# Local attention on one Trainium2 core: turning and weighing of the probabilities moved one unit behind the scores, exponentials taken from PSUM with the maximum as bias

## The reference

```
def _layer(x, wqkv, qs, ksc, wo, lg, lb, w1, b1, w2, b2):
    h = shift_token(x)
    qkv = h @ wqkv
    q, k, v = jnp.split(qkv, 3, axis=-1)
    ...
    q = l2norm(q) * qs
    k = l2norm(k) * ksc
    q, k = rotary_xpos(q, k)
    o = local_attention(q, k, v)      # softmax(q k^T * 8 + mask) v, over own and previous window
    ...
    x = x + o @ wo
    h = shift_token(x)
    ...                               # layer norm of h
    h = h @ w1 + b1
    a, g = jnp.split(h, 2, axis=-1)
    h = a * jax.nn.gelu(g, approximate=False)
    x = x + h @ w2 + b2
    return x
```

## Time and profile before

| what | us |
|---|---|
| three timed runs | 1561.47, 1565.78, 1570.25 (median 1565.78) |
| the profiled execution, its own time | 1563.58 |
| its span, first to last instruction | 1561.7 |
| steady attention of layer 0, of layer 1 (about) | 750 to 1017, 1167 to 1433 |
| busy PE, DVE, ACT, POOL | 1346.8, 1145.6, 801.7, 724.0 |

### The profile page before, as it was taken

One profiled execution on the slowest core, in us unless ns is written; L12 is line 12 of the kernel. 1 busy time (PEld: TensorE's weight loads), 2 busy tenths in 40 slices (PEclk: granted clock), 3 DMA queues, 4 the chain that ended last, 5 costly groups with the idle time before them and its releaser, 6 DMA issues.

```text
span 1561.7 us, 39029 instructions
## 1 busy us (share of the span) xinstructions
PE 1346.8 (86%) x15968; PEld 970.4 (62%) x15968; DVE 1145.6 (73%) x2484; ACT 801.7 (51%) x1633; POOL 724.0 (46%) x562
## 2 busy tenths in 40 slices
PE   4545999988999999984999999967989999998797
PEld 3434878875777777762666666654556666665554
DVE  3776776434888888874888888864578888888565
ACT  1222223224666666653777777742457777776421
POOL 1752545541344433434666666632246666666100
PEclk7776999996999999997999999999999999999999
DMA  4000544500000000003000100011100000000011
GB/s 133 0 0 16 112 93 110 108 13 2 3 3 3 4 3 3 3 3 91 8 8 7 22 8 8 1 30 28 25 24 8 9 17 13 9 5 2 12 31 54
DMA packets 61837, 40.34 MB, mean 26 GB/s; under 512 B 41312, under 2 KB 51808, under 8 KB 61664
## 3 DMA queue, kind: packets, MB, share of 16 engines
q1 hardware_dynamic: 61664, 37.88, 10.2%
HBM read 27.12 MB, written 2.36 MB: 19 GB/s over the span
## 4 chain that ended last, share of the span: by engine, by line
PE 33%; ACT 8%; SPq 6%; DVE 4%; POOL 2%; issue 1%; DMA 1%; DVEq 0%; POOLq 0%; ACTq 0%
PE PS L1872 7%; SPq L1463 5%; PE PS L1923 5%; PE PS L1957 4%; PE PS L1914 4%; PE PS L1891 3%; PE PS L1937 2%; ACT e_oT L1787 2%; PE PS L1948 2%; ACT qk L1756 2%; ACT e_pm L1793 2%; PE PS L1907 2%; POOL rot L1537 2%; PE PS L2010 1%; PE PS L2019 1%
## 5 line engine op out<-in xcount | busy, mean ns | idle before, releaser
L1537 POOL TENSOR_TENSOR rot<-qk,sinl 128x1024 f32<-128x1024 f32 x64 | 217.6, 3401 | 139.4 <-DVE qk L1631 139.4
L1530 POOL TENSOR_TENSOR rn<-ss,neghalf 128x16 f32<-128x16 f32 x64 | 185.6, 2901 | 108.6 <-DVE ss L1624 108.6
L1756 ACT ACTIVATE qk<-PS 128x512 f32<-128x512 f32 x128 | 76.4, 597 | 135.7 <-PE PS L1872 135.7
L1102 DVE TENSOR_REDUCE d_mx<-PS 128x4 f32<-128x576 f32 x128 | 96.9, 757 | 66.3 <-PE PS L1246 63.3
L1872 PE MATMUL PS<-wqkv,hT 128*128 128x512 f32 x256 | 128.8, 626 | 10.9 <-DMA qks<-in_e_ks 5.7
L607 POOL TENSOR_TENSOR uu<-uu,cb 128x512 f32<-128x512 f32 x64 | 82.8, 1295 | 90.0 <-DVE uu L839 88.2
L1923 PE MATMUL PS<-ident,e_pm 128*128 128x128 f32 x512 | 84.5, 289 | 45.9 <-ACT e_pm L1793 44.3
L1923 PEld LDWEIGHTS PS<-ident,e_pm 128*128 128x128 f32 x512 | 55.9, 144 | 102.4 <-ACT e_pm L1793 95.7
L739 ACT ACTIVATE sg<-PS 128x512 f32<-128x512 f32 x72 | 43.0, 597 | 134.1 <-PE PS L667 133.0
L1165 ACT ACTIVATE pa<-PS 128x512 f32<-128x512 f32 x128 | 76.5, 597 | 61.8 <-PE PS L1255 61.7
L1610 DVE TENSOR_REDUCE e_mx<-PS 128x8 f32<-128x1024 f32 x64 | 78.2, 1222 | 30.7 <-PE PS L1914 30.6
(11 more groups left out here) (241 smaller groups left out, 3535.9 us busy)
## 6 DMA issues: line engine op xcount, KB each, us to landing
cb<-comb_rows SPq DMA_DIRECT2D x32, 512.0 KB, 9.1
X<-in_L_attn_x SPq DMA_DIRECT2D x4, 512.0 KB, 7.4
zs<-Z SPq DMA_DIRECT2D x64, 32.0 KB
zg<-Z SPq DMA_DIRECT2D x16, 128.0 KB
out_x<-X SPq DMA_DIRECT2D x8, 256.0 KB, 2.5
zs<-Z SPq DMA_DIRECT2D x64, 31.8 KB
zg<-Z SPq DMA_DIRECT2D x16, 127.0 KB
wqkv<-in_e_wqkv SPq DMA_DIRECT2D x2, 768.0 KB, 4.2
```

Of the source, the lines that this page charges most:

```text
L1102: chain(dve.tensor_reduce(mx[:, par, :, :], s, AX.X, ALU.max))
L1530: pool.tensor_tensor(rn[:, v % 2, :], ss[:, v % 2, :], c.neghalf[:, :], ALU.pow).then_inc(rn_ready.sem, 1)
L1537: pool.tensor_tensor(rot[:, :, :, :], x, bc(sinl[:, t, :, :], 2, H2), ALU.mult).then_inc(rot_ready.sem, 1)
L1756: last = act.activation(qk[:, v % 4, s, :, :].rearrange("p h e -> p (h e)"), PS[:, QBANK + s, :], ACT.Copy)
```

## The change

The work of a unit on PE after its scores moves one step later. In step u, PE now turns and weighs the probabilities of unit u - 1 (`turn_p`, `weigh`) and turns and projects the output of unit u - 2 (`turn_o`, `project_o`); the v projection is of unit u + 2. DVE's `divide` and `resid_sum` and ACT's `take_p`, `take_o` and `values` move with them. The order within the step also changes: the first `turn_p` stands between the q/k projection and the v projection, the second before `turn_qk`.

DVE no longer subtracts. It writes the negated maxima into a buffer of two (`maxima`), and ACT's `exponent` reads the scores from PSUM and adds the negated maximum as its bias. Since a bias is one number per partition and each of the eight heads of a row has its own, this takes eight activations of 128 columns a unit, where there were two of 512. They stand in four pairs between ACT's other work. The banks of the scores are free once the last exponential has read them (`p_exp`), where before it was the last subtraction.

ACT's copies of q and k are signalled one by one, and `features` of the next unit stands ahead of `squares`. Each layer gets one more step, `attend(L, nunits)`, and the first hidden projection `up(L, 0, 0)` moves to its head.

```
@@ dve @@
-                def shift(L, v):
+                def maxima(L, v):
                     dve.wait_ge(s_ready.sem, s_ready.at(n(L, v)))
+                    if n(L, v) > 2:
+                        dve.wait_ge(p_exp.sem, p_exp.at(2 * (n(L, v) - 2)))
                     s = PS[:, SBANK:SBANK + 2, :].rearrange("p r (j k) -> p r j k", k=2 * W2)
-                    steps(dve.tensor_reduce(mx[:, :, :], s, AX.X, ALU.max))
-                    for h in range(2):
-                        if n(L, v) > 2:
-                            dve.wait_ge(pT_psum.sem, pT_psum.at(2 * (n(L, v) - 2) - 1 + h))
-                        dve.tensor_tensor(pm[:, v % 2, h, :, :, :], s[:, :, 2 * h:2 * h + 2, :],
-                                          bc(mx[:, :, 2 * h:2 * h + 2], 3, 2 * W2), ALU.subtract).then_inc(p_shifted.sem, 1)
+                    dve.tensor_reduce(mx[:, v % 2, :, :], s, AX.X, ALU.max, negate=True).then_inc(max_ready.sem, 1)
...
@@ act @@
-                def exponent(L, v, h):
-                    act.wait_ge(p_shifted.sem, p_shifted.at(2 * n(L, v) - 1 + h))
-                    p = pm[:, v % 2, h, :, :, :].rearrange("p r j k -> p (r j k)")
-                    act.activation(p, p, ACT.Exp).then_inc(p_exp.sem, 1)
+                def exponent(L, v, h, r):
+                    if h == 0 and r == 0:
+                        act.wait_ge(max_ready.sem, max_ready.at(n(L, v)))
+                    if n(L, v) > 2 and r == 0:
+                        act.wait_ge(pT_psum.sem, pT_psum.at(2 * (n(L, v) - 2) - 1 + h))
+                    for j in range(2):
+                        at = 2 * h + j
+                        last = act.activation(pm[:, v % 2, h, r, j, :], PS[:, SBANK + r, at * KEYS2:(at + 1) * KEYS2], ACT.Exp,
+                                              bias=mx[:, v % 2, r, at:at + 1])
+                    if r == 1:
+                        last.then_inc(p_exp.sem, 1)
...
                 def attend(L, u):
                     if has(u + 4):
-                        if u >= 0 or L == 0:
-                            features(L, u + 4)
-                        take_features(L, u + 4)
+                        take_features(L, u + 4, 0)
                     if has(u):
-                        exponent(L, u, 0)
-                        exponent(L, u, 1)
-                        take_p(L, u, 0)
-                    if has(u + 3):
-                        values(L, u + 3)
+                        exponent(L, u, 0, 0)
+                    if has(u + 4):
+                        take_features(L, u + 4, 1)
+                    if has(u - 1):
+                        take_p(L, u - 1, 0)
...
@@ pe, scores @@
                     if v >= 1:
-                        pe.wait_ge(p_shifted.sem, p_shifted.at(2 * n(L, v - 1)))
+                        pe.wait_ge(p_exp.sem, p_exp.at(2 * n(L, v - 1)))
...
@@ pe, end of a layer @@
                     for u in range(nunits):
                         attend(L, u)
-                    up(L, 0, 0)
+                    attend(L, nunits)
                     turn_o(L, nunits - 1)
                     project_o(L, nunits - 1)
```

More of the change, by code:

```diff
@@ L1646, in attend @@
                     if has(u):
-                        shift(L, u)
+                        maxima(L, u)
                     if u == nunits - 3:
@@ L1656, in attend @@
                         square_sums(L, u + 3)
-                    if has(u):
-                        divide(L, u, 0)
+                    if has(u - 1):
+                        divide(L, u - 1, 0)
                     if has(u + 2):
@@ L1662, in attend @@
                         clamp(L, u + 3)
-                    if has(u):
-                        divide(L, u, 1)
                     if has(u - 1):
-                        resid_sum(L, u - 1)
+                        divide(L, u - 1, 1)
+                    if has(u - 2):
+                        resid_sum(L, u - 2)
                 def stats(L, g):
@@ L1751, in features, with take_features @@
                     act.activation(h_of(v), PS[:, QBANK, 0:P], ACT.Copy).then_inc(eh_ready.sem, 1)
[L1753 to L1757, removed]
+                def take_features(L, v, s):
+                    act.wait_ge(eqkv_ready.sem, eqkv_ready.at(2 * n(L, v) - 1 + s))
+                    act.activation(qk[:, v % 4, s, :, :].rearrange("p h e -> p (h e)"), PS[:, QBANK + s, :],
+                                   ACT.Copy).then_inc(qk_taken.sem, 1)
                 def squares(L, v):
-                    act.wait_ge(qk_taken.sem, qk_taken.at(n(L, v)))
+                    act.wait_ge(qk_taken.sem, qk_taken.at(2 * n(L, v)))
                     if n(L, v) > 1:
@@ L1800, in attend @@
                     if has(u + 4):
-                        if u >= 0 or L == 0:
-                            features(L, u + 4)
-                        take_features(L, u + 4)
+                        take_features(L, u + 4, 0)
                     if has(u):
-                        exponent(L, u, 0)
-                        exponent(L, u, 1)
-                        take_p(L, u, 0)
-                    if has(u + 3):
-                        values(L, u + 3)
+                        exponent(L, u, 0, 0)
+                    if has(u + 4):
+                        take_features(L, u + 4, 1)
+                    if has(u - 1):
+                        take_p(L, u - 1, 0)
+                    if has(u):
+                        exponent(L, u, 0, 1)
+                    if has(u + 2):
+                        values(L, u + 2)
                     if u == nunits - 1:
                         whole(L, 0)
+                    if has(u - 1):
+                        take_p(L, u - 1, 1)
                     if has(u):
-                        take_p(L, u, 1)
-                    if has(u - 1):
-                        take_o(L, u - 1)
+                        exponent(L, u, 1, 0)
+                    if has(u - 2):
+                        take_o(L, u - 2)
+                    if has(u):
+                        exponent(L, u, 1, 1)
                     if has(u + 1):
                         take_qk(L, u + 1)
+                    if has(u + 5) and (u >= -1 or L == 0):
+                        features(L, u + 5)
                     if has(u + 4):
@@ L1834, in gelu @@
                        .then_inc(gelu_ready.sem, 1)
+                features(0, 0)
                 for L in range(DEPTH):
@@ L1964, in attend @@
                         project_qk(L, u + 4)
-                    if has(u + 3):
-                        project_v(L, u + 3)
+                    if u == nunits:
+                        up(L, 0, 0)
+                    if has(u - 1):
+                        turn_p(L, u - 1, 0)
+                    if has(u + 2):
+                        project_v(L, u + 2)
                     if u == nunits - 1:
                         turn_x(L, 0)
-                    if has(u):
-                        turn_p(L, u, 0)
+                    if has(u - 1):
+                        turn_p(L, u - 1, 1)
                     if has(u + 1):
                         turn_qk(L, u + 1)
-                    if has(u):
-                        turn_p(L, u, 1)
-                        weigh(L, u, 0)
                     if has(u - 1):
-                        turn_o(L, u - 1)
-                    if has(u):
-                        weigh(L, u, 1)
+                        weigh(L, u - 1, 0)
+                    if has(u - 2):
+                        turn_o(L, u - 2)
                     if has(u - 1):
-                        project_o(L, u - 1)
+                        weigh(L, u - 1, 1)
+                    if has(u - 2):
+                        project_o(L, u - 2)
                     if has(u + 5):
```

12 lines of the change are left out of this document (6 added, 6 removed).

## The result

The changed kernel takes 1572.03 us (median of 5 runs, 1570.54 to 1574.15); the kernel before takes 1565.19 (5 runs, 1561.47 to 1570.25). The ratio is 1.0042, 95% interval 1.0021 to 1.0062. So it is slower, as forecast, but by 0.4% where my 1583 is 1.1% above the 1565.8 of before; the rise in spans is 1571.8 - 1561.7 = 10.1 us against 18.6. The time lies in my wide range of 1556 to 1601, but under the forecast's own 1574 to 1592, in the band that I had given to the break-even.

What follows compares the result with a forecast made beforehand. A loop through PE and ACT's copies, with PE nearly full, sets the 9.85 us period; 16.4 + 3.2 - 1.0 = +18.6 on 1563.6 gives 1582.2, stated as 1583 us; own range 1574 to 1592, wide range 1556 to 1601.

Steps and rivals of the forecast that it cites:

- the break-even: Rival case: pair of exponentials near 0.4 us and changes of kind cheap, +0.05 a unit, about 1569 us; chance 0.18.
- the loop: PE from projection to output turn, ACT's copies of oT, qT, kT, then PE's z, mask, scores, next projection; sets the period.
- Part (a): DVE loses two subtractions, 1.29 us, and keeps the maximum, 1.23; costed at nothing in steady units.
- Part (b): On ACT, eight 128-column exponentials with bias replace two of 512: 0.26 us apart, 0.52 a pair, bounds 0.31 and 0.73.
- Part (c): PE regains 0.46 us from the exponential's wait, pays 0.25 for the new order; output turn at 5.60 instead of 5.81.
- rival 4: First p's copy comes late and PE stalls at the second turn; 0.3 slip gives +0.1 a unit; no separate chance.
- Part (d): Last pair of exponentials on ACT delays qT, kT and PE's z: 0.52 - 0.21 = 0.31 a unit, +16.4 us.
- Part (e): Features moved ahead of the squares on ACT cost nothing; the v projection one unit later changes no sum.
- Part (f): Ends of a layer: 44.0 us before, 45.6 after, +1.6 a layer, give or take 3.
- Minus 1.3 and plus 5.5: Layer's end, us each: unit 31 to first hidden projection -1.3; first to second hidden projection +5.5.
- Rival 1: Removed wait wins between oT copy and z turn: -0.15 us a unit, with ends about 1550 us; chance 0.12.

Runs made afterwards that it cites:

- the order alone: The changed kernel's order on all engines, but with DVE's subtraction and two 512-column exponentials as in the kernel before; 1537.07 us, ratio 0.981 to the kernel before.
- fewer changes: Against the changed order with DVE's subtraction and two 512-column exponentials: v projection before first turn of p, second turn after turns of q and k; 1543.69 us, ratio 0.986.

## Why the prediction was off

- *The bound, the loop and the direction: right.* The copies behind the output turn set the period; moving one pair across the copy of oT moves it by 0.51 us (two experiments). From the output turn to the next unit's projection it takes 4.04 us before and 4.05 in every kernel with no pair behind the oT copy (for the order alone 869.66 - 865.61), 4.56 with one pair there and 5.07 with two. So the period is the place of the output turn, plus 4.05, plus the pairs behind it.
- *Part (a), DVE at nothing: right in the steady units.* The order alone, with the subtractions, is the faster by 0.65 us a unit. What DVE was relieved of was not on the path there.
- *Part (b), 0.26 apart, 0.52 a pair: right.* It measured 0.25 and 0.50; one takes 0.38 us. By the formula of the Trainium skill (ScalarE: Activation LUTs, What ACT_TABLE_LOAD costs) one was estimated at 0.39, which the trace bears out; with its overlap of 0.09 the estimate of a pair was 0.59, which was high: the overlap seen here is 0.13.
- *Part (c), the head start of the output turn: the step that failed.* It was forecast at 0.46 - 0.25 = 0.21 us (5.81 to 5.60) and measured 0.36 (5.45). Both terms were off.
  - *The wait taken away, put at 0.46, is worth 0.58.* The kernel of the section on fewer changes has the PE order of before and no wait for an exponential, and its output turn is at 5.23. From v to the first turn of p it takes 863.58 - 862.72 = 0.86 where it took 1.37, and I had taken 0.91 for the pace; the other 0.07 is the turn itself, which took 0.50 to the next start right behind the wait and takes 0.43 without one.
  - *The price of changes between wide passes and transposes, put at 0.25, is not there.* From four turns of p to the wide v projection it is 883.53 - 883.09 = 0.44. The 0.08 that I read from four turns of the output (0.58 to the next start) belongs to the passage to the weighing products, which both orders have. What the changed kernel does lose against 5.23 is 0.22, and it is a wait that I had excluded ("No other wait gets in before it"): the second turn of p starts at 884.67, 0.14 after ACT's copy of the first is written (883.91 + 0.62 = 884.53), and 1.14 behind v instead of 0.86. The order alone has the same wait, but shorter: the turn starts at 863.56, again 0.14 after its copy (862.83 + 0.59 = 863.42), and 0.99 behind v. The profile puts neither in brackets; the same 0.14 or 0.15 stands at this place in all five kernels with this order that were read. The copy ends at 3.26 of the unit, as I had said (3.3), but PE is there at 1.82 + 0.44 + 0.86 = 3.12 and not at 3.5, because my price was not paid. That 0.25 lies near 0.22 is luck. My rival 4 named that place. In the order alone the copy is written at 3.11; in the changed kernel the first pair of exponentials stands ahead of the second q/k copy, and so of this one. This last part is read from rows; no kernel moved that pair alone.
- *Part (d), +0.31 a unit: too large by that term.* -0.36 for the turn and +0.50 for the pair are +0.14, as measured (+0.15). In the steady units the mistake is 16.4 - 8.0 = 8.4 of the 8.5 us by which I was out. On top of the new order, the exponentials cost 0.65: 0.50 for the last pair and 0.15 for the later copy of the first p.
- *Part (e): right, as far as the rows show.* ACT is still idle 1.30 us before its next q/k copy (1.83 before).
- *Part (f), the ends: right where the queue was walked, wrong where it was left.* Minus 1.3 and plus 5.5 came as forecast to 0.2 us, but I had not followed the delay further. From there to layer 1's unit 2, and to the end, 1.8 and 2.5 us of it come back; which wait of the feed-forward part takes them up I have not traced. And units 28 to 31 won less than expected: in layer 0 the three steps take 9.11, 11.32 and 10.54 us where I had 9.6, 11.1 and 9.1. These errors cancel by luck: outside of the steady units 0.6 + 1.5 = 2.1 us were measured, 2.2 forecast.
- *The sum.* The profiled execution is 2.2 us under the median, and 1582.2 + 2.2 is 1584.4; the recorded 1583 takes in only a part of it. Rival 1's own numbers likewise give 2 to 4 us more than its 1550.
- *Rivals.* Break-even was nearest in time: the turn is early by 0.36, as it supposed, but the pair costs 0.50 and not 0.4. The removed wait does win 0.50 us a unit (order alone), more than rival 1 allowed, but not together with the pair behind the oT copy.

## What to carry over

Moving work one unit behind its producer pays if the consumer was waiting for it: here 0.50 us of 9.85 a unit. But an engine that is far from full can still set the period: look for the copy for which the busiest engine waits last, and keep every added instruction out of the stretch between its operands' arrival and that copy; the idle time just ahead of it is free. Read a wait on PE from starts, since the time in brackets counts from a modelled end: 0.34 there was 0.50. And measure a suspected price of a sequence at the very pair of operations that the new order will have, not at a similar one.

## What the runs showed of the hardware

- An exponential of 128 columns with a bias pointer, from PSUM, takes 379 ns and the next starts 0.25 us later. Eight of them take 2.17 us in a row, two of 512 columns 1.14.
- PE passes from float32 transposes to a 512-column projection after 0.44 us for four, the pace of transposes to transposes (0.43 and 0.46), at full clock (1.00 in the stretch, 2.4 GHz). From four transposes of p to the weighing products it takes 0.55 (865.51 - 864.96 in the kernel with fewer changes).
- With 97.8 of 98.5 us PE was nearly without idle time in the order alone, at the same granted clock of 1.00.
- After PE had been idle for 2.28 us at the end of layer 0 in the kernel with fewer changes, its granted clock over the next 4.85 us was 0.65; after 0.34 us of idle time at the same place in the order alone it stayed at 1.00.
